# Two attention layers with feed-forwards: norms moved behind their products, one-part score maxima, and a last batch worked in two token halves

## What is computed

```python
x = x + L0_xattn(_layernorm(x), ctx_768)      # 16 heads of width 8, logits clipped to +-1e4, softmax, Wo, bo
x = x + L0_ffn(_layernorm(x))                 # square(relu(xf @ Ws1)) @ Ws2, plus experts times trunc(routing weight)
x = x + L1_xattn(_layernorm(x), ctx_768)      # one head of width 128: q = n @ Wq + bq, softmax(q k^T) v
x = x + L1_ffn(_layernorm(x))                 # softmax(xf @ Ws + bs); each of 8 experts takes its 256 best tokens of all 2048
```

## Time and profile before

| | us |
|---|---|
| median of 3 runs (lowest to highest) | 259.44 (259.16 to 260.93) |
| profiled execution, device time | 258.55 |
| its span, from the first to the last instruction in the trace | 256.7 |
| PE / PEld / DVE / ACT / POOL busy in the span | 214.2 / 125.6 / 154.3 / 91.7 / 84.1 |
| chain that ended last: PE, DVE, POOL, issue, DMA, ACT | 36%, 33%, 11%, 8%, 5%, 5% |

### The profile page before, as it was taken

How to read it: one execution, slowest core, us unless ns; L and a number is a source line. 1 busy time by engine, 2 the same in 40 slices (tenths; PEclk the granted TensorE clock), 3 DMA queues, 4 the chain that set the end, 5 groups by cost and what they waited for, 6 DMA issues and landing times.

```text
span 256.7 us, 3638 instructions
## 1 busy us (share of the span) xinstructions
PE 214.2 (83%) x1260; PEld 125.6 (49%) x1269; DVE 154.3 (60%) x545; ACT 91.7 (36%) x196; POOL 84.1 (33%) x91
## 2 busy tenths in 40 slices
PE   1797589998799969999999997899877898888860
PEld 0543245335353645357544664564323676777750
DVE  5998836609968999568565846668878171111110
ACT  3151056352441644146502142224673433332330
POOL 2248407000107011102110413030005478888653
PEclk9999999999999999999999999999999999999996
DMA  7501111001100005961100101021001133323322
GB/s 212 175 9 23 46 48 52 20 3 46 36 1 4 0 0 179 323 197 46 42 0 3 43 0 42 0 87 45 0 0 28 29 43 42 46 39 39 41 24 27
DMA packets 15194, 13.09 MB, mean 51 GB/s; under 512 B 3520, under 2 KB 12161, under 8 KB 15169
## 3 DMA queue, kind: packets, MB, share of 16 engines
q1 hardware_dynamic: 11440, 10.17, 12.6%
q0 software_dynamic: 3008, 2.31, 6.8%
q10 hardware_dynamic: 721, 0.30, 0.4%
HBM read 7.99 MB, written 3.21 MB: 44 GB/s over the span
## 4 chain that ended last, share of the span: by engine, by line
PE 36%; DVE 33%; POOL 11%; issue 8%; DMA 5%; ACT 5%; POOLq 1%; DVEq 0%; ACTq 0%
PE psum L907 7%; POOL out L1661 6%; PE psum L820 6%; DVE rden L1290 5%; DVE mrow L1269 5%; DMA out<-pT,idx 4%; DVE xn L1222 4%; DVE stats L1213 3%; DVE pT L1431 3%; POOL pT L1653 2%; PE psum L830 2%; PE psum L889 2%; POOL rstd L1594 2%; PE psum L863 2%; PE psum L932 2%
## 5 line engine op out<-in xcount | busy, mean ns | idle before, releaser
L707 ACT ACTIVATE pT<-psum 103x512 f32<-103x512 f32 (+1 forms) x48 | 28.4, 597 | 45.0 <-PE psum L891 44.9
L820 PE MATMUL psum<-c 128*128 128x512 bf16 x170 | 41.9, 379 | 0.5
L1593 POOL TENSOR_SCALAR ve<-mv 128x4 f32<-128x4 f32 (+1 forms) x19 | 4.4, 229 | 94.5 <-DVE mv L1216 94.5
L1269 DVE TENSOR_REDUCE mrow<-psum 128x4 bf16<-128x308 f32 x64 | 27.4, 469 | 5.1 <-PE psum L863 4.6
L1661 POOL DMA_INDIRECT out<-pT,idx x16 | 25.5, 1595 | 11.7 <-DVE pT L1498 6.5
L1653 POOL DMA_INDIRECT pT<-gather_rows,idx x16 | 17.0, 1060 | 28.8 <-DVE idx L1485 24.5
L1496 DVE TENSOR_TENSOR pT<-psum,b_rows 128x256 f32<-128x256 f32 (+1 forms) x9 | 3.5, 393 | 36.7 <-PE psum L1169 36.7
L820 PEld LDWEIGHTS psum<-c 128*128 128x128 bf16 x179 | 17.1, 99 | 15.9 <-issue 0.6
L863 PE MATMUL psum<-k_stack,q_stack 128*128 128x308 f16 x64 | 16.7, 299 | 7.2 <-DVE mrow L1269 6.8
L668 ACT COPY xnT<-psum 128x512 f32<-128x512 f32 (+1 forms) x19 | 9.8, 517 | 28.2 <-PE psum L830 28.1
L1157 PE MATMUL psum<-xinT,w 128*128 128x256 f32 (+1 forms) x72 | 16.3, 369 | 3.9 <-ACT xinT L776 3.9
(11 more groups left out here) (181 smaller groups left out, 369.4 us busy)
## 6 DMA issues: line engine op xcount, KB each, us to landing
w<-in_L_ffn_W SPq DMA_DIRECT2D x16, 256.0 KB, 5.6
gather_rows<-xrow SPq DMA_DIRECT2D x4, 272.0 KB, 2.1
x<-in_x SPq DMA_DIRECT2D x4, 256.0 KB, 4.1
out<-res SPq DMA_DIRECT2D x4, 256.0 KB, 2.0
q_stack<-q_hi SPq DMA_DIRECT2D x24, 32.0 KB, 1.8
q_stack<-q_lo SPq DMA_DIRECT2D x24, 32.0 KB, 1.8
b_rows<-in_L_ffn_b SPq DMA_DIRECT2D x1, 512.0 KB, 3.4
pT<-gather_rows,idx POOLq DMA_INDIRECT x16, 2.7
```

The source lines that it names most:

```text
L707: nc.scalar.activation(pT[0:n, b % 2, s, :], ST_ps[s % 2][0:n, :], ACT.Exp).then_inc(exp_done, 1)
L820: pe.matmul(bank[b][:, :], ident16, c16[:, 0:4 * P], start=True, stop=True)
L1269: dve.tensor_reduce(mrow[:, b % 2, j, g * GH:(g + 1) * GH], S_ps[u % 2][:, 0:GK].rearrange("p (h k) -> p h k", h=GH), X, ALU.max).then_inc ...
```

## The change

- **Maxima.** The shift of the exponent needs no exact maximum, so it is taken from the high parts only: `scores` multiplies 32 rows of `q_hi` by 32 rows of a masked key copy `k_max`, two groups side by side in two row tiles of the array, into two banks. `maxima` reduces both at once: 32 reductions of 616 instead of 64 of 308. For batches 0 and 1 two pairs of banks take turns (`score_bank`); for later ones there is one pair.
- **Head.** One query product (`prep_q(0)`), the same split as for the other batches, and the stack of batch 0 filled by 16 small transfers, 8 from SP, 4 from ACT and 4 from POOL. Keys of batch 0 come first (`k4_first`), those of the others later. The sign and scale are in per-row constants, so the low keys take one DVE operation each time. POOL masks `k_max` and normalises batch 1. PE has 11 early fill products.
- **Norms behind products.** For norms 1 to 3 the raw stream is turned. Weights are centred once (`centre` times `Ws1`, `Ws`, and `Wq` times the keys: `w_c`, `key_map`, `key_bias`), so that the mean drops out, and the scale is applied to the product: `gain1` (one over the variance) in `add_shared`, `rstd` in `scale1` and `scale2`. The query product of layer 1 is gone. The rows that the experts gather are normalised on POOL (`rows`).
- **Shared feed-forward.** Two halves of tokens in two column tiles, then two row tiles; ACT's two operations are half as long. The layer-0 router product and its MAX8 are gone; the flag tests the spread of the router's weights instead.
- **Layer-1 softmax.** Four exponentials with bias and sum on ACT in place of one; DVE subtracts and sums no more.
- **Last batch.** `scores_T` and `attend` of batch 3 work on one half of the tokens, then on the other, in phase 3; the layer-1 steps of batch `ph-2` end in their phase; phases 4 to 6 are replaced by one list per engine, written out by hand.
- **Start of the experts.** The first gather goes out after one count (`idx_first`); the fill of 20 products is split in 4 and 7.

The core of the diff (`scores`, `attend_half`, the functions of the norms, the lists behind the loop):

```diff
-        S_ps, ST_ps = bank[0:2], bank[2:4]
+        ST_ps = bank[2:4]
+        att_ps = [tail1_ps] * (B - 1) + [bank[0:2]]
+        def score_bank(b, u):
+            return (2 * (u % 2), 5 * (u % 2))[b] if b < 2 else 0
@@ PE
-            def scores(b, j, groups=range(G)):
-                for g in groups:
-                    u = (b * J + j) * G + g
-                    if u >= 2:
-                        if b == 0:
-                            warm_head(1)
-                        pe.wait_ge(max_done, u - 1)
-                    pe.matmul(S_ps[u % 2][:, 0:GK], q_stack[:, b, g, j * P:(j + 1) * P],
-                              k_stack[:, b, g].rearrange("p h k -> p (h k)"), start=True, stop=True).then_inc(s_ps_done, 1)
+            def scores(b, u):
+                if u == 0:
+                    pe.wait_ge(q_hi_done, b + 1)
+                    pe.wait_ge(k_max_done, 1 if b == 0 else 2)
...
+                    pe.wait_ge(max_done, PAIRS + max(u - 1, 0))
+                elif b >= 2:
+                    pe.wait_ge(max_done, b * PAIRS + u)
+                elif u >= 2:
+                    warm_head(3)
+                    pe.wait_ge(max_done, u - 1)
+                j, g0, to = u // 2, u % 2 * 2, score_bank(b, u)
+                for k in range(2):
+                    rows = slice((g0 + k) * GD, (g0 + k + 1) * GD)
+                    pe.matmul(bank[to + k][:, 0:GK], q_hi[rows, b % 2, j * P:(j + 1) * P], k_max[rows, b].rearrange("p h k -> p (h k)"),
+                              start=True, stop=True, tile_position=((g0 + k) * GD, 0)).then_inc(s_ps_done, 1)
+            def attend_half(half, c):
+                n, of = chunk_rows(c), slice(half * HT, (half + 1) * HT)
+                for to, by in ((den_ps, value_mask), (O_ps, None)):
+                    for g in range(G):
...
+            def residual_T(n, t, u, ps, j0=0, j1=J):
+                pe.wait_ge((None, res1_done, res2_done, res3_done)[n], u + 1)
+                transposes(n, t, ps, j0, j1)
...
+            def scores1(t, u, j0, j1, ps):
+                pe.wait_ge(xnT_done[2], u + 1)
+                for j in range(j0, j1):
+                    ins = pe.matmul(ps[:, j * NK:(j + 1) * NK], xnT[:, 2, j * P:(j + 1) * P], key_map[:, t, :], start=True, stop=True)
@@ DVE
-                    dve.tensor_reduce(mrow[:, b % 2, j, g * GH:(g + 1) * GH], S_ps[u % 2][:, 0:GK].rearrange("p (h k) -> p h k", h=GH),
-                                      X, ALU.max).then_inc(max_done, 1)
+                dve.tensor_reduce(mrow[:, b % 2, u // 2, h0:h0 + 2 * GH].rearrange("p (c h) -> p c h", c=2),
+                                  psum[:, to:to + 2, 0:GK].rearrange("p c (h k) -> p c h k", h=GH), X, ALU.max).then_inc(max_done, 1)
+            def add_shared(t, u, j0, j1, ps):
+                dve.wait_ge(ffn_ps_done, 2 * (u + 1))
+                dve.wait_ge(rstd_done[1], u + 1)
+                for j in range(j0, j1):
+                    ins = dve.scalar_tensor_tensor(res[:, t * J + j, :], of, gain1[:, t * J + j:t * J + j + 1],
+                                                   res[:, t * J + j, :], ALU.mult, ALU.add)
+            def scale1(t, u, j0, j1, ps):
+                for j in range(j0, j1):
+                    ins = dve.scalar_tensor_tensor(p1[:, j], ps[:, j * NK:(j + 1) * NK], rstd[:, 2, j:j + 1], key_bias[:, t, :],
+                                                   ALU.mult, ALU.add)
+                settle(ins)
+                dve.tensor_reduce(m1[:, t % 2, j0:j1], p1[:, j0:j1], X, ALU.min).then_inc(sub1_done, 1)
@@ DVE, behind the loop
+                add_projection(B - 1, ua, a0, a1, aps)
+                stats1(B - 1, ua, a0, a1)
+                normalise(B - 1, ub, b0, b1_)
+                scale1(t, t, 0, J, tail2_ps)
+                add_projection(B - 1, ub, b0, b1_, bps)
+                stats1(B - 1, ub, b0, b1_)
+                add_shared(B - 1, ua, a0, a1, aps)
+                stats2(B - 1, ua, a0, a1)
...
@@ POOL, head
+            ln_rstd(0, 0, 0)
+            mask_keys(0, 1)
+            ln_rstd(0, 1, 1)
...
+            pool.wait_ge(q_lo_done, 1)
+            for g in range(G):
+                pool.dma_start(q_stack[3 * GD:, 0, g, :], q_lo[g * GD:(g + 1) * GD, 0, :]).then_inc(q_stack_low, 16)
+            pool.wait_ge(k_lo_done, 1)
+            stack_keys(0)
@@ PE, experts
-                    warm(20, 5)
+                    warm(7, 5)
```

More of the change, by code:

```diff
@@ new lines, in hidden, with shared @@
+            def hidden(u, j0, j1, ps):
+                pe.wait_ge(xnT_done[1], u + 1)
+                jm = (j0 + j1) // 2
+                for k, (ja, jb) in enumerate(((j0, jm), (jm, j1))):
+                    pe.matmul(ps[1][k * F0:(k + 1) * F0, j0 * P:jm * P], w_c[:, 0:F0], xnT[:, 1, ja * P:jb * P], start=True, stop=True,
+                              tile_position=(0, k * F0)).then_inc(hid_ps_done, 1)
+            def shared(u, j0, j1, ps):
+                pe.wait_ge(hid2_done, u + 1)
+                jm = (j0 + j1) // 2
+                for j in range(j0, jm):
+                    for k in range(2):
+                        rows = slice(k * F0, (k + 1) * F0)
+                        ins = pe.matmul(ps[1 - k][:, j * P:(j + 1) * P], hid2[rows, j * P:(j + 1) * P], w_s2[rows, :], start=True, stop=True,
+                                        tile_position=(k * F0, 0))
+                        if j == jm - 1:
+                            ins.then_inc(ffn_ps_done, 1)
@@ L941, in _ @@
-            for j in range(J):
-                scores(0, j)
-                if j == 0:
+                ins = pe.matmul(k4_first[:, g, :], w_k4[:, g].rearrange("p r d -> p (r d)"), ctxT[:, 0, 0:NK], start=True, stop=True)
+            ins.then_inc(k4_ps_done, 1)
+            prep_T(0)
+            keys_later(0)
+            pe.wait_ge(ld_q0, 16)
+            prep_q(0)
+            keys_later(1).then_inc(k4_ps_done, 1)
+            pe.wait_ge(ld_c16, 16)
+            pe.wait_ge(k_lo_done, 1)
+            for u in range(PAIRS):
+                scores(0, u)
+                if u == 3:
@@ new lines, in _ @@
+            t = B - 2
+            attend_half(1, 2)
+            residual_T(1, B - 1, ua, aps[0], a0, a1)
+            pe.wait_ge(sub2_done, t)
+            scores1(t, t, 0, J, tail2_ps)
+            warm(1, 3)
+            hidden(ua, a0, a1, aps)
+            warm(3, 3)
+            project(ub, b0, b1_, bps)
+            warm(1, 3)
+            shared(ua, a0, a1, aps)
+            warm(2, 3)
+            residual_T(1, B - 1, ub, bps[0], b0, b1_)
+            warm(2, 3)
+            weights1_T(t, 0, J, tail2_ps)
@@ L1121, in indices @@
                 for g, (e0, e1) in enumerate(INDEX_GROUPS):
+                    if g == 2 and not again:
+                        warm(4, 5)
                     pe.wait_ge(cumx_done, again * len(INDEX_GROUPS) + g + 1)
@@ L1322, in _ @@
[L1322 to L1328 removed]
+                keys_low(0, 1, k4_first.rearrange("p (u g) k -> p u g k", g=2))
@@ L1338, in _ @@
-                for ph in range(B + 3):
+                dve.wait_ge(ld_bq, 16)
+                q_low(0)
+                for u in range(PAIRS):
+                    maxima(0, u)
+                for ph in range(B):
                     b = ph
                     for s in range(SLOTS):
-                        if b < B and s == 0:
+                        if s == 0:
                             maxima_out(b)
+                            if b == 0:
+                                q_low(1)
+                                ln0_apply(2)
+                            if b == 1:
+                                ln0_apply(3)
```

1098 lines of the change are left out of this document (627 added, 471 removed).

## The result

The changed kernel takes 218.53 us (median of 4 runs, 217.69 to 219.9) where the one before takes 259.47 in the same comparison: a ratio of 0.842, with an interval of 0.837 to 0.847. Forecast were 217 and a range of 208 to 230. The profiled execution has a span of 215.8 us (forecast 214.1), a second one 216.5. The device times of single executions lie 1.9 us above their spans, as before.

A forecast was written before the change was run, and what follows sets the result against it. The prediction took a chain hopping between engines as the bound, with the experts bound by POOL. Its terms summed to -42.6 us: span 214.1, 216.0 with time outside it, forecast median 217, range 208 to 230.

The forecast's parts named there:

- Head: Start to last turn of batch 0's maxima: earlier first maximum, eight reductions of 0.75 us; -12.5 us, to 19.2.
- The tie with the stack: Head: batch 0's stack transfers land near 19 us, level with the maxima, with 2 us at risk.
- Phase 0: Up to batch 1's last turn of maxima: DVE's list about 12.7 us, one stall about 1.5; -3.2, to 14.6.
- Phase 1: Up to batch 2's last turn of maxima: 10.9 us of remaining DVE work, about a microsecond of stalls; -2.1, to 26.6.
- Phase 2: Up to batch 3's last turn of maxima: the 3.89 us pass goes, the reciprocal waits for denominators; -2.3, to 24.8.
- Phase 3: Up to the last attention product: PE's list decides, about 8.3 us gone and 0.9 added; -6.8 us.
- Behind the attention: Last attention product to first search count: DVE work falls to 21.6 us, one list replaces waiting phases; -14.0, to 24.4.
- POOL's `rows`: POOL's new pass: 1.6 us for four tiles, covered by DVE's list; without that cover 3 to 4 us.
- Search to first product: First search count to first expert product: the fill ends 1.8 us earlier, less one small test; -1.7, to 22.6.
- the slow chain: Rival, 226 us: costlier hops, `rows` blocks DVE or precedes roots, phases 1 and 2 gain nothing; chance 0.22.
- its opposite: Rival, 209 us: less overlap lost than charged, phases 1 and 3 end with PE's work, hops cost nothing; chance 0.14.
- The clock: Rival, 232 us: TensorE falls to 1.2 GHz for half of phase 0's and the tail's work, +15; chance 0.12.

The follow-up runs named there:

- run 1: The changed kernel with one pair of banks, not two, for the maxima of batches 0 and 1: 229.46 us.
- run 12: run 9 without six fills ahead of the last turn of batch 0's maxima, and with seven ahead of batch 1's: 214.99 us, 0.825 of the kernel before.
- run 8: The changed kernel with batch 1's turn later in the head, batch 3's a slot earlier, POOL's residual and key stack of batch 2 in phase 0: 219.37 us.
- run 9: run 8 without PE's wait for the key map and the five fills behind it in phase 1: 216.49 us.
- run 5: run 4 with fill products on PE ahead of every turn that waits for a norm pass: 250.54 us.
- run 6: The changed kernel with POOL's four passes that normalise the experts' rows moved back to DVE: 220.0 us.
- run 11: The changed kernel with the old fill of 20 products before the first gathered rows, in place of four and seven: 224.16 us.
- run 3: The changed kernel without the 31 fill products between the last attention product and the search: 223.4 us.
- run 4: The changed kernel with ten passes of norms 1 and 2 put back on DVE, PE's turns waiting for them: 264.98 us, ratio 1.018.

## Why the prediction was right, step by step

The total was right to 1.5 us, partly because errors cancelled: the head and phases 1 and 3 were 1.45, 1.7 and 0.6 late, the stretch behind the attention 2.3 early.

- **Head, -12.5 forecast, -11.0 and -11.9 measured.** The first maximum came at 13.06 and 12.16 (forecast about 12.1). Of the 0.90 us between the two, 0.2 is the landing of the tokens (4.26 and 4.03); POOL's first root took 1.33 us in place of 1.05, and DVE's pass behind it, part of it beside POOL's mask of `k_max`, 1.50 in place of 1.11. The steps of 0.73 to 0.75 us held. "Two pairs of banks keep DVE fed" is shown by run 1, but 8 x 0.75 left out that PE's list also carries the turn and the query of batch 1, the first held by POOL's pass up to 14.99 (3.15 us, where the norm pass on DVE took 1.12): gaps of 0.36 and 1.04 us. The tie with the stack was no limit: in run 12 the turned maxima come 0.9 us earlier, counted from the first reduction.
- **Phase 0, forecast 14.6, measured 14.83.** Right. Run 1 shows the second pair of banks works here too: without it 1.9 us are lost.
- **Phase 1, -2.1 forecast, -0.4 measured.** The product of the reciprocal ended at 50.16, 14.7 us into the phase (forecast 14.3 to 15). The step that failed is "about a microsecond of stalls" for the rest: it lasted 13.65 us with 10.61 of DVE's work, so 3.0 of stalls. Batch 2 has one pair of banks, and each step is 1.2 us where nothing else fills it. The pass over batch 3, 2.87 us for 1.1, was not in my list. Runs 8, 9 and 12 show what stood in line: high part, key map with its fills, and the clock.
- **Phase 2, 24.8 forecast and measured.** The total is right, by two small errors: the reciprocal starts 4.1 us into the phase (forecast 3.6, before 4.6), and the rest takes 20.7 (forecast 21.2). That the pass of 3.89 us was POOL's doing is shown again in run 5, where one put back there took 3.38 beside POOL's residual and key stack.
- **Phase 3, 25.0 forecast, 25.58 measured.** PE's list decides, as forecast: 24.90 busy.
- **Behind the attention, 24.4 forecast, 22.12 measured.** Mis-sized twice. DVE's list was put at 21.6 us and is 18.98, part of it lying ahead of the last attention product; and hops cost nothing that shows, for DVE idles 3.1 us in all. Run 5 gives 7.2 us of the gain of 16.3 to the norms, as an upper bound, run 6 gives 2.6 to POOL's rows, and half of the reciprocal with its product, 2.2, now runs in phase 3. The other 4.3 or more (the query product, sums, MAX8, the order of the lists) was not taken apart: no run puts the phases back in place of the one list, and none puts back the 64 reductions.
- **POOL's `rows`.** 3.2 us, not 1.6: the estimate from two neighbours, both with two inputs and one of them in 16 bits, failed for this form. It was harmless, as DVE's cover held; DVE waited for a root for 0.8 us in all.
- **Search to first product, -1.7 forecast.** The stretch lost 2.2, of which the fill is 1.8 (run 11).
- **Rivals.** Neither 226 nor 209 came, but a part of each did: phase 1 gained next to nothing, as the slow chain has it, and hops cost nothing behind the attention, as its opposite has it. The clock did not fall ahead of the experts in the changed kernel, but the runs show how near it is: in the profiles of eight of the eleven edited kernels some stretch ahead of the experts is below 1.00, and the cost went from 1 to 2 us (the better executions of run 3) to 14 to 22 (run 4). I gave it the smallest chance but one, and it decides most of the runs. The busy share that I named for phases 2 and 3, 92% and more, is 91% in phase 2 (24.75 of 27.12 us).

## What to carry to other kernels

Where engines run in-order lists, an operation that another list waits for costs what is queued behind the waiter, here 2.7 us on average for a pass that is mostly 0.6 to 1.2; count that, and name what is late next, before an edit is priced. Compare versions stage by stage from an event inside the stage, not from the start of the program, since its first microseconds vary: the first reduction came at 12.1 to 15.8 us. Fill products are worth their place in PE's waits and cost in full ahead of an instruction that is due: put them where PE would stand anyway, and look at the granted clock first whenever a small edit costs more than its own length.

## What the runs showed of the hardware that I had not expected

- TensorE fell to 1.2 GHz without any long gap: in run 1 from 15 us on, after gaps of 0.25 to 0.86 us; in run 3 from 126 us on, after gaps of 0.2 to 1.12 us. The same list of instructions kept its clock in one execution and lost it in another (run 8 and run 9 at the start of phase 1).
- POOL takes 798 ns for a 128x128 float32 `tensor_scalar` with two scalars per row, where DVE takes 0.34 us. In the changed kernel all five passes took 3.14 to 3.16 us.
- One DVE operation of 0.33 us took 2.10 beside a POOL operation that had started 0.24 us earlier. DVE's operations that read PSUM kept their length beside POOL's 3.15 us pass: L1449 took 0.90 for four at 115.97, as it did at 99.09 and 75.24.
